# Feed-forward products of a decoder layer, issued in pairs of tiles

## The reference

```python
xq = activation_quant(rms_norm(x))          # rows scaled to steps of max/127 and rounded
g = jax.nn.silu(ternary_matmul(xq, W_g))    # x @ sign(W_g).T, 512 -> 2048
u = ternary_matmul(xq, W_u)
p = g * u
return ternary_matmul(p, W_d)               # 2048 -> 512
...
x = _layernorm(x + _L0_ffn_ref(x, L0_ffn_W_g, L0_ffn_W_u, L0_ffn_W_d), axis=-1)
```

## Time and profile before

| | before |
|---|---|
| median of 3 runs | 1622.2 us (1622.14 to 1622.71) |
| span of the profiled execution | 1621.2 us; 1.0 us of the median lies around it |
| busy TensorE / VectorE / ScalarE / GpSimd | 1574.0 / 1014.8 / 788.7 / 286.4 us |
| feed-forward stage in the span | about 1363 to 1621 us |
| longest waits of TensorE's matmuls in it | `y_bank` for `prod_lo` 2.5 us in 5 times; `g_bank` for a product 2.2 us in 5 times |

### The profile page before, as it was taken

One profiled execution on the slowest core, in us unless ns is written; L12 is line 12 of the kernel. 1 busy time (PEld: TensorE's weight loads), 2 busy tenths in 40 slices (PEclk: granted clock), 3 DMA queues, 4 the chain that ended last, 5 costly groups with the idle time before them and its releaser, 6 DMA issues. The chain is left out here.

```text
span 1621.2 us, 25726 instructions
## 1 busy us (share of the span) xinstructions
PE 1574.0 (97%) x8332; PEld 1270.9 (78%) x8352; DVE 1014.8 (63%) x2125; ACT 788.7 (49%) x1789; POOL 286.4 (18%) x301
## 2 busy tenths in 40 slices
PE   8999999999999999999999999997999998999997
PEld 7888888888888888888888888885887775565564
DVE  4555555555555555555555555567899996877854
ACT  5444444444444444444444444444888875433332
POOL 0000000000000000000000000004788872433432
PEclk9999999999999999999999999997999999999998
DMA  5000010100101001010010100011111100000000
GB/s 175 29 31 19 26 32 14 44 19 26 32 13 45 19 26 32 13 42 22 26 32 13 32 32 26 2 45 47 52 58 59 40 20 1 1 27 1 26 26 27
DMA packets 40393, 50.85 MB, mean 31 GB/s; under 512 B 3488, under 2 KB 19872, under 8 KB 40352
## 3 DMA queue, kind: packets, MB, share of 16 engines
q1 hardware_dynamic: 40352, 50.35, 9.7%
HBM read 46.14 MB, written 4.19 MB: 31 GB/s over the span
## 5 line engine op out<-in xcount | busy, mean ns | idle before, releaser
L162 POOL TENSOR_TENSOR norm_rstd<-norm_var_eps,minus_half 128x4 f32<-128x4 f32 x12 | 12.2, 1014 | 1116.2 <-DVE norm_var_eps L122 1116.2
L645 DVE SCALAR_TENSOR_TENSOR acc<-attn_bank,prob_recip,acc 128x512 f32<-128x512 f32 x256 | 179.7, 744 | 16.9 <-PE attn_bank L487 16.9
L510 ACT ACTIVATE probs<-probs,neg_max 128x128 f32<-128x128 f32 (+3 forms) x256 | 142.0, 557 | 61.7 <-DVE neg_max L590 61.7
L581 DVE TENSOR_TENSOR zT_lo<-attn_bank,zT_hi 128x512 fp32r<-128x512 f32 x64 | 44.3, 692 | 190.0 <-ACT zT_hi L504 190.0
L504 ACT CAST kT_hi<-attn_bank 128x512 fp32r<-128x512 f32 x64 | 37.5, 587 | 180.3 <-PE attn_bank L355 180.3
L581 DVE TENSOR_TENSOR qT_lo<-attn_bank,qT_hi 128x512 fp32r<-128x512 f32 x64 | 44.2, 691 | 126.0 <-ACT qT_hi L504 125.9
L581 DVE TENSOR_TENSOR kT_lo<-attn_bank,kT_hi 128x512 fp32r<-128x512 f32 x64 | 44.3, 692 | 122.9 <-ACT kT_hi L504 122.9
L1195 PE MATMUL y_bank<-wdT_f32r,prod_hi 128*128 128x512 f32 x256 | 110.8, 433 | 3.0 <-POOL prod_lo L1136 2.5
L1136 POOL TENSOR_TENSOR prod_lo<-prod,prod_hi 128x512 fp32r<-128x512 f32 x64 | 85.6, 1337 | 142.1 <-ACT prod_hi L1244 142.1
L590 DVE CUSTOM_DVE_ANT_0 probs<-attn_bank,mask 128x128 f32<-128x128 f32 (+3 forms) x256 | 109.8, 485 | 0.1
L487 PE MATMUL attn_bank<-woT_hi,zT_hi 128*128 128x512 f32 x256 | 106.2, 415 | 1.6 <-DVE zT_lo L581 1.4
(11 more groups left out here) (149 smaller groups left out, 4176.1 us busy)
## 6 DMA issues: line engine op xcount, KB each, us to landing
rows_twice<-in_ctx_dram SPq DMA_DIRECT2D x64, 128.0 KB, 2.6
rows<-in_L_attn_W_K_dram SPq DMA_DIRECT2D x16, 256.0 KB, 2.6
rows<-in_L_attn_W_Q_dram SPq DMA_DIRECT2D x16, 256.0 KB, 2.9
rows<-in_L_attn_W_V_dram SPq DMA_DIRECT2D x16, 256.0 KB, 3.4
rows<-in_L_attn_W_O_dram SPq DMA_DIRECT2D x16, 256.0 KB, 2.7
rows_twice<-in_L_ffn_W_g_dram SPq DMA_DIRECT2D x16, 256.0 KB, 2.7
rows_twice<-in_L_ffn_W_u_dram SPq DMA_DIRECT2D x16, 256.0 KB, 2.8
rows_twice<-in_L_ffn_W_d_dram SPq DMA_DIRECT2D x16, 256.0 KB, 2.7
```

Source lines behind the costliest of these rows:

```text
L510: nc.scalar.activation(probs[:, cols], probs[:, cols], ACT.Exp, bias=low[:, par, t:t + 1], scale=-1.0, accum_out=total[:, par, t:t + 1]).t ...
L581: nc.vector.tensor_tensor(parts[1][:, at:at + cols], bank[:, 0:cols], parts[0][:, at:at + cols].bitcast(F32), ALU.subtract).then_inc(done, 1)
L645: nc.vector.scalar_tensor_tensor(out=acc[:, b * NT + t, :], in0=O_BANK[t][:], scalar=recip[:, par, t:t + 1], in1=acc[:, b * NT + t, :], op ...
```

## The change: TensorE's order in the feed-forward loop

The loop over tiles goes in steps of two: the gate-up passes of two tiles stand together, and then the down passes of two tiles. The steps at the end of a batch keep their places between down 13, down 14 and down 15. Nothing else is edited.

```diff
-                    for t in range(NHT):
+                    for t in range(0, NHT, 2):
                         if t + 2 < NHT:
                             gate_up(b, t + 2)
-                        if t == NHT - 2 and not last:
+                            gate_up(b, t + 3)
+                        elif not last:
                             turn_x(b + 1, False)
                         down(b, t, first)
                         if t == NHT - 2 and not last:
                             spread_steps(b + 1)
+                        down(b, t + 1, first)
```

## The result

Median 1625.91 us (8 runs, 1622.58 to 1627.94) against 1620.69 for the kernel before in the same sessions (8 runs, 1618.60 to 1622.71). The ratio is 1.0029, with a 95% interval of 1.0017 to 1.0040: 4.7 us, between 2.8 and 6.5 (the two medians lie 5.2 apart). The two profiled spans differ by 4.3 us (1625.5 against 1621.2). The prediction was 1626.2, or 4.0 above the 1622.2 of before that it had.

What follows compares the result with a forecast made beforehand. TensorE, busy 97% of the span, was taken to bound the kernel. New waits less vanished ones gave +4.45 us, less 0.4 for switches: about +4.0 on 1622.2, so 1626.2, range 1621.5 to 1629.

Steps and rivals of the forecast that it cites:

- Odd gate-up passes: Odd passes 3 to 15, issued 1.87 us earlier, wait for VectorE's products, up to 1.50 us; likeliest case, 59%.
- Down passes: In tiles 11 to 15, waits for `prod_lo` go: 1.24 us in batch 0, 1.52 in each middle batch.
- Switches: On TensorE, 28 fewer changes from down to gate-up pass give back 0 to 0.56 us, taken as 0.4.
- ScalarE and the end: silu(t+1) queues behind hi(t), covered by 1.3 us; at the last batch's end a wait of some 0.6 stays.
- Sum: Batch 0 +0.55, batches 1 and 2 +1.45 each, batch 3 +1.00, less 0.4: about +4.0 us.
- That the passes would not wait: Rival: odd gate-up passes meet no wait, so only old waits and switches go, 5.4 us faster, 1616.8; 12%.
- Cancelling: Rival: over the feed-forward batches, gains and new waits about balance, 1622.2 to 1625; 22%.
- one fall of the clock: Rival: new TensorE waits lower its clock, each fall taking 3.4 us; 1629.6 at one, 1646.6 at six; 7%.

Runs made afterwards that it cites:

- pairs_light: Pair order with VectorE's norm and quantiser operations in the tile loop cut to 32 of 512 columns; 1616.65 us, ratio 0.9967 to before.
- pairs_only_2: Kernel before with one of seven steps paired (gate-up 4 and 5, then down 2 and 3); 1623.72 us, ratio 1.0011 to before.
- pairs_spread: Pair order with VectorE's norm and quantiser operations placed more evenly over the tiles, nothing left out; 1619.22 us, ratio 0.9992 to before.
- start_pair_late: Kernel before with rounding moved to tile 13, spread of steps to tile 14, and each batch's first step paired; 1617.72 us, ratio 0.9981 to before.
- single_late: Kernel before with only the rounding moved from tile 12 to 13 and the spread of steps from 12 to 14; 1618.54 us, ratio 0.9987.

## Why the prediction was right, step by step

**Odd gate-up passes**, the main term: predicted waits 1.18, 1.50, 0.47 and 0.25 before gate-up 5, 11, 13 and 3; measured 1.16, 1.49, 0.49 and 0.26. pairs_light and pairs_only_2 show the cause, VectorE's work between gate and product. What makes that work so long was not asked. In batch 1 of after one of the four copies takes 1.49 in norm 3's apply and 1.50 in the quantiser norm's, against 0.53 to 0.55 for the others, both with a `prod_lo` beside them. An estimate from these rows: without the collision products 3 and 9 would start 0.95 sooner, and the waits before gate-up 5 and 11 would be 0.2 and 0.5. No run has the pair order and the old placement with a short `prod_lo`, so how much of the loss is the collision's stays open.

**Down passes:** the waits of 1.24 and 1.52 went. The reason that the prediction gave for the odd ones was loose: down 11 has the same passes ahead of it in both orders. What changed is when TensorE comes for it. In before that was 2.76 after the start of product(11) (1470.38 to 1473.14), and the `prod_lo` of 2.26 us opened it at 3.80. In after gate-up 11 and 13 had already waited 1.98, and TensorE came at 1472.67 + 1.73 + 1.87 = 1476.27, 4.34 after product(11), when `prod_lo` was long done. The prediction took the old wait as a number and did not ask what made it. The waiting of tiles 11 to 15 is 1.52 in the one order and 1.98 in the other, so the quantiser's part of the loss is only 0.46 a batch; norm 3's 1.16 is new altogether.

**Switches:** taken at 0.4. An undisturbed pair of tiles takes 7.19 (1447.37 to 1454.56 in after) against 2 x 3.60, so 28 give 0.3.

**ScalarE and the end:** silu(15) did stand behind hi(14), and VectorE idled 2.1 us for it, without a wait on TensorE in the middle batches. From U(15) to the last matmul's start the last batch takes 8.67 in after (1605.73 to 1614.40), of which 0.86 + 4 x 1.87 - 0.23 = 8.11 is work: a wait of 0.56, where 0.6 was predicted to stay.

**Sum:** +0.55, +1.45, +1.45, +1.00 less 0.4 was predicted, so 0.45, 1.35, 1.35 and 0.90 with the switches shared out; +0.55, +1.40, +1.40, +0.85 came. The measured ratio says 4.7, with 4.0 inside its interval.

**The rivals.** That the passes would not wait was excluded by the rows above. Cancelling (+0.5 to below 3.2) is not excluded by the interval of 2.8 to 6.5 alone, but by the batches, which are 4.2 longer and show the waits. The clock of the middle batches stayed at 1.00 through waits of 1.5 us. The rule of the Trainium skill ("TensorE: Matmul & The Clock Gate", A second HAM failure mode: psum-queue depth-cycling) is not borne out by idles of this size: no middle batch of the twelve traces is below 1.00. The price that the prediction put on one fall of the clock, 3.4 us, was too high as well: traces with and without the fall at the stage's start differ by 2.6 (last section).

## What to carry to other kernels

Grouping passes on the bound engine moves their deadlines even when nothing is added: list for each pass what frees its buffer, and how much earlier or later it is asked for. A pass asked for one slot earlier must be checked against the longest burst of in-order work in front of its producer, here 5.9 us of norm work in two tiles (the 7.74 from gate(8) to product(9), less two gates and a product of about 0.6 each from start to start). After a change of order, work that was placed by hand for the old order has to be placed anew, and measured, since splitting it can cost more than its even spread brings. And when a pass waits for one engine, look at what runs beside that engine's work: before down 11 the wait was GpSimd's, and moving VectorE's rounding took it away.

## What the runs showed of the hardware

VectorE's copies with scale and offset from SBUF to SBUF take 0.53 us for 128x512 alone and up to 1.6 when a GpSimd operation runs beside them; neither its gates and products, which read PSUM (0.67 to 0.69 in every timeline read), nor its statistics (2.46 for four) are touched. In batch 1 of pairs_spread seven of the eight long copies ended 0.28 to 0.29 us after the `prod_lo` beside them. It also goes the other way: in before the four rounding copies beside `prod_lo` of tile 11 took 0.41 each, undisturbed, and `prod_lo` took 2.26 in place of 1.28. What decides which of the two waits these traces do not tell. The Trainium skill ("GPSIMD Engine Reference", Specifications) says that GpSimd's interfaces to SBUF are shared with VectorE and that they contend with VectorE's instructions in a two-port mode or with two SBUF inputs. The traces agree that they contend, and put the price at about 1 us a collision; no view shows in which mode the copies run.

The scatter of the whole time has a source in this stage. TensorE idles 2.2 us before the first `turn_x` in every trace. In before the clock fell behind it, as in nine other traces; in the profiled executions of pairs_only_2 and start_pair_late it did not (windows of pairs_only_2, same columns; the clock is the third value from the right):

```profile
1354.60:1356.60 2.00, 0.61 (x3) 0.18 (x1) 2.00 (x8) 0.00 (x0) 0.00 (x0) 1.00 0.00 0
...
1360.60:1362.60 2.00, 1.48 (x7) 0.71 (x8) 0.00 (x0) 1.66 (x2) 0.00 (x0) 1.00 0.00 0
```

From the first `turn_x` to the second it took 59.88 us, against 62.47 in before: 2.6 us that go with the fall of the clock, in a batch where the two kernels should take the same time. start_pair_late against single_late says the same (58.97 and 61.61, of which some 0.2 is the pairing). It is not the only source: well ahead of this stage the granted clock was 0.51 from 1111 to 1120 us and 0.50 from 1130 to 1138 us in before, and 0.81 and 0.93 in start_pair_late, and the first `turn_x` came at 1358.85 and 1356.80 us, though nothing ahead of it differs between the two. How much of that is the clock's was not tested. This scatter is why stretches of the trace tell these kernels apart better than single executions do.
